# Attention: the result of each batch leaves by four indirect scatters from POOL in place of one plain store from SP

## Chip, cores and metric

The kernel runs on one core of one Trainium2 chip. The metric is device time in microseconds, the median of the runs shown; lower is better. One core has five engines that run their own lists of instructions and meet at semaphores: PE (TensorE, matmuls), DVE (VectorE), ACT (ScalarE), POOL (GpSimd) and SP (SyncE, which here only issues transfers). Transfers issued from SP and from POOL go through different queues to the same 16 DMA engines.

## What is computed

A block of a network on x of shape (16, 512, 128): half a mixture-of-experts step, attention, half a mixture-of-experts step, each on a layer norm of x and added to x. The change touches only the attention step:

```python
x = x + 0.5 * ffn(layernorm(x))          # 8 experts, top 2, and a shared one
x = x + attn(layernorm(x))
x = x + 0.5 * ffn(layernorm(x))

def attn(x, ...):                        # 16 heads of 8
    q, k, v = (x @ W.T + b for each of Wq, Wk, Wv), split by heads
    a = softmax(q k^T / sqrt(8)) * head_mask
    return (a v) @ Wo.T + bo
```

## The kernel before

The kernel is one program with three stages after a setup: `ffn1`, `attention` (L1052) and `ffn2`. Each stage goes over the 16 batches of 512 rows. Between the stages the rows lie in DRAM, in `after_ffn` and `after_attn`; a batch there is seen as 128 partitions of 4 consecutive rows (`dst_b`, L1094), so that one store moves 2 KB per partition.

In attention a batch is 16 **units** (4 quads of heads times 4 tiles of 128 rows), and a unit has two halves. For each half PE computes a pair of score tiles for the exponents (`score_exp`, L1179, rows L1187) and, 8 units ahead, a pair for the row maxima (`score_max`, L1193, rows L1201); DVE reduces the latter to maxima (`take_max`, L1482, rows L1489) and ACT takes the exponents (`exponential`, L1338, rows L1341). The maxima of a quad (group g) must be subtracted before the exponents. They are put into extra rows of the packed q operand: POOL splits them (`split_max`, L1417, rows L1423 and L1425), PE turns them (`turn_max`, L1224, rows L1227), ACT copies them out (`copy_max`, L1332, rows L1335), and POOL issues two small transfers that put them into `q_pack` (`pack_max`, L1428, rows L1432). PE waits for these transfers before the first unit of the group, in `batch` of PE (L1257):

```python
if u % NT == 0:
    g = u // NT
    pe.wait_ge(max_packed[g % 2], ...)
```

The order of every engine is written out by hand: `pieces` of PE (L1272), ACT (L1373) and DVE (L1535) and `batch` of POOL (L1441) name what goes into which unit. Work that belongs to the end of a batch is done in the early units of the next one. There, with a the batch before and b the present one: DVE normalises the last quad of a (unit 2), PE turns it and multiplies by Wo (units 3 and 4, rows L1242 and L1248), and DVE adds `x_bias` (the attention's input plus bo) and writes `x_out` (`residual`, L1506, rows L1510, unit 4). Then POOL makes the `x_bias` of b (`add_bias`, L1435, rows L1438) and packs the maxima of group 2. PE's bank `p_x` is used by many steps in turn; the semaphore `x_bank_drained` counts its uses.

SP's list for a batch (L1152) loads x for two batches on (`front.load_in`, row L344), loads the rows that the residual needs (`load_res`, row L1146), issues the packed operands of the next batch (rows L351 and L357), and last stores a (`store`, L1148, row L1150) when its residual has drained the bank. Two buffers `x_out` alternate; the residual waits until the store of two batches before has landed (`stored`, L1509). The last store follows the last residual; SP waits for all stores (L1173) before the stage is left, and all engines meet there.

Of the kernel before, what the change touches and what calls it, by code (L numbers as in the profile page):

```python
# [14 lines left out]

F32 = mybir.dt.float32
F32R = mybir.dt.float32r
BF16 = mybir.dt.bfloat16
ALU = mybir.AluOpType
ACT = mybir.ActivationFunctionType  # L20
# [2 lines left out]
P = 128  # L23
# [5 lines left out]
S = 512  # L29
NT = S // P  # L30
NB = 16
# [53 lines left out]
def need(eng, sem, value):  # L85

    if isinstance(value, int) and value <= 0:
        return
    eng.wait_ge(sem, value)
# [17 lines left out]
def every_batch(eng, batch):  # L107

    for k in range(NB):
        batch(Turn(0, k), k == 0, k == NB - 1)  # L110


def setup(nc, dram, w, feed):
# [5 lines left out]
    with ExitStack() as ctx:  # L119
# [27 lines left out]
        @block.sync  # L147
        def _(sp):
            feed.load_in(sp, begin)
            feed.load_in(sp, second)  # L150
            sp.dma_start(w.gate_w[:], dram["gate_w_t"]).then_inc(gate_w_loaded, 16)
            sp.dma_start(w.rank[:], dram["rank"]).then_inc(rank_loaded, 16)
            for dst, routed, shared, loaded in ((gate, dram["w_gate"], dram["sw_gate"], gate_loaded),
                                                (up, dram["w_up"], dram["sw_up"], up_loaded)):
                sp.dma_start(dst[:, 0:ROUTED], routed).then_inc(loaded, 16)
                sp.dma_start(dst[:, ROUTED:HID], shared).then_inc(loaded, 16)
            sp.dma_start(wq[:], dram["wq_t"]).then_inc(qk_loaded, 16)
            sp.dma_start(wk[:], dram["wk_t"]).then_inc(qk_loaded, 16)
            sp.dma_start(w.wv[:], dram["wv_t"]).then_inc(attn_loaded, 16)
            sp.dma_start(wo[:], dram["wo_t"]).then_inc(attn_loaded, 16)  # L160
            sp.dma_start(mask_rows[:], dram["head_mask"].rearrange("(p a) -> p a", a=1)).then_inc(attn_loaded, 16)
            sp.dma_start(w.bq[:], dram["bq"].rearrange("(p a) -> p a", a=1)).then_inc(attn_loaded, 16)
            sp.dma_start(w.bk[:], dram["bk"].rearrange("(p a) -> p a", a=1)).then_inc(attn_loaded, 16)
            for dst, name in ((w.bv, "bv"), (w.bo, "bo")):
                sp.dma_start(dst[:], dram[name].rearrange("(a n) -> a n", a=1)
                             .to_broadcast([P, dram[name].shape[0]])).then_inc(attn_loaded, 16)
            sp.wait_ge(attn_loaded, 16 * 7)

        @block.tensor
        def _(pe):  # L170
# [44 lines left out]
        @block.vector  # L215
        def _(dve):
            nc.vector.memset(w.minus_half[:], -0.5).then_inc(half_set, 1)
            nc.vector.memset(w.selector[:], 0.0).then_inc(selector_cleared, 1)
            feed.norm_stats(dve, begin)
            feed.norm_stats(dve, second)  # L220
            for part in range(3):
                feed.norm_var(dve, begin, part)
            for n, (_, _, full, high, low) in enumerate(splits):
                dve.wait_ge(high_done, n + 1)
                nc.vector.tensor_tensor(low, full, high.bitcast(F32), ALU.subtract).then_inc(low_done, 1)
                if n == 0:
                    dve.wait_ge(ident_loaded, 16)
                    dve.wait_ge(consts_loaded, 16)
                    nc.vector.tensor_copy(w.ident16[:], w.ident[:])
                    dve.wait_ge(selector_cleared, 1)  # L230
                    nc.vector.tensor_copy(w.selector[0:PARTS * E, :], selector[:])
                if n == 1:
                    dve.wait_ge(rank_loaded, 16)
                    for part in range(feed.EARLY_PARTS):
                        feed.route(dve, bank, begin, part)
            dve.wait_ge(attn_loaded, 16 * 7)
            nc.vector.tensor_scalar(w.wo[:], wo[:], mask_rows[:], None, ALU.mult)
            dve.wait_ge(low_done, len(splits))

# [812 lines left out]
def attention(nc, w, front, feed, src, dst):  # L1052
# [9 lines left out]
    with ExitStack() as ctx:  # L1062
# [76 lines left out]
        @block.sync  # L1139
        def _(sp):  # L1140
            def load_res(b):

                need(sp, exp_tile, b.count(PAIRS))
                sp.dma_start(x_res[b.par][:], b.of(src_b)).then_inc(x_res_loaded[b.par], 16)  # L1146

            def store(b, drained):  # L1148
                sp.wait_ge(x_bank_drained, drained)
                sp.dma_start(b.of(dst_b), x_out[b.par][:]).then_inc(stored[b.par], 16)  # L1150

            def batch(b, is_first, is_last):  # L1152
                a, c = b.step(-1), b.step(1)
                if there(b, 2):
                    front.load_in(sp, b.step(2))
                load_res(b)
                if is_last:
                    for n in following:
                        sp.wait_ge(stored[n.par], 16)
                        feed.load_in(sp, n)  # L1160
                if there(b, 1):
                    for n in range(len(PRODUCTS)):
                        front.pack_block(sp, c, "q", n)
                        front.pack_block(sp, c, "k", n)
                    front.clear_max_rows(sp, c)
                if not is_first:
                    store(a, uses(b, "out") + 1)

            end = Turn(0, NB - 1)
            every_batch(sp, batch)  # L1170
            store(end, last_uses + 3)
            for par in range(2):
                sp.wait_ge(stored[par], 16 * NB // 2)  # L1173

        @block.tensor
        def _(pe):
# [237 lines left out]
        def _(pool):  # L1414
# [20 lines left out]
            def add_bias(b, drained):  # L1435
# [2 lines left out]
                G.tensor_tensor(x_bias[:], x_res[b.par][:], w.bo[:].unsqueeze(1).to_broadcast([P, NT, D]),  # L1438
                                ALU.add).then_inc(bias_ready, 1)

            def batch(b, is_first, is_last):  # L1441
                a, c, e = b.step(-1), b.step(1), b.step(2)
                split_max(b, 1, 0 if is_first else uses(a, "m3") + 1)
# [6 lines left out]
                    front.scale(pool, e, 5 if is_first else uses(a, "x") + 1)  # L1450
                split_max(b, 2, uses(a, "m0") + 1 if not is_first else FIRST_USES.index("m0") + 1)
                add_bias(b, 0 if is_first else uses(b, "out") + 1)
                pack_max(b, 2, uses(b, "m2") + 1)
                split_max(b, 3, uses(b, "m1") + 1)
                pack_max(b, 3, uses(b, "m3") + 1)
# [10 lines left out]
                if there(e):  # L1466
                    front.operand_low(pool, e, "k")

            begin = Turn(0, 0)
            split_max(begin, 0, 0)  # L1470
            pack_max(begin, 0, FIRST_USES.index("m0") + 1)
            every_batch(pool, batch)

        @block.vector
        def _(dve):
# [30 lines left out]
            def residual(b, n):  # L1506
                dve.wait_ge(x_bank_filled, n + 1)
                dve.wait_ge(bias_ready, b.count(1, 1))
                need(dve, stored[b.par], b.half(16))  # L1509
                V.tensor_tensor(x_out[b.par][:], p_x[:].rearrange("p (t d) -> p t d", d=D), x_bias[:],  # L1510
                                ALU.add).then_inc(x_bank_drained, 1)

# [52 lines left out]
class Weights:  # L1565


    def __init__(self, nc, ctx):
# [15 lines left out]
        self.values = [sb(f"values{i}", [P, NT, HEADS, COLS]) for i in range(2)]  # L1584
        self.zeros = sb("zeros", [P, QUAD, NT])
        self.zero_rows = sb("zero_rows", [QUAD, S])


def program(nc, dram, out):
# [51 lines left out]
```

## Time and profile before

| | us |
|---|---|
| median of 3 runs | 1906.76 |
| lowest and highest | 1904.23, 1912.45 |
| span of the profiled execution | 1899.1 |
| median less that span | 7.66 |
| PE, DVE, ACT, POOL busy | 1755.1, 1391.1, 1237.0, 891.2 |

The profiled execution's own time is given by its span, from its first to its last instruction; what lies around it is the fourth line. How rows are read: in an **order of time** a row is start (us), busy time (us), engine, line of the kernel, operation, out<-in, shape, count of merged instructions, and in brackets the idle time of the engine before it and what ended that. A row of **windows** gives for a stretch its length, the busy time and count of PE, PE's weight loads, DVE, ACT and POOL, then the granted clock of PE (1.00 is 2.4 GHz), the share of the DMA engines and GB/s. A row of **DMA issues** gives the issuing queue, the count, the size of each and the median time from issue to landing. A row of a **line** gives minimum, median and maximum duration in ns, and first and last start. A row of **groups** gives count, busy us, mean ns, and idle time before. SPq rows are issues on SP's queue.

### The profile page before, as it was taken

The numbers are of one execution on the slowest core, as the hardware profiler recorded it, in microseconds if no ns is written. First come the engines' busy times: TensorE is split into PE (matmuls) and PEld (weight loads), VectorE is DVE, ScalarE is ACT, GpSimd is POOL, SyncE is SP. The second block draws the span as 40 slices with busy tenths as digits, with TensorE's granted clock in tenths as the row PEclk, the third lists the DMA queues.
The fourth block names the chain that finished last, engine by engine and source line by source line (L and its number), as shares of the span: only waits on it lengthen the run. The fifth ranks groups of instructions, "written<-read, shape, count | busy, mean of one in ns | idle before, by whom it ended". The sixth has DMA issues, their size and how long they took to land. (4 is left out here: it accounts for less than half of the span.)

```text
span 1899.1 us, 30193 instructions
## 1 busy us (share of the span) xinstructions
PE 1755.1 (92%) x9569; PEld 1100.5 (58%) x9600; DVE 1391.1 (73%) x2393; ACT 1237.0 (65%) x1914; POOL 891.2 (47%) x878
## 2 busy tenths in 40 slices
PE   5999999999968888888888888888889999999999
PEld 4887878787843333333333333333368787878776
DVE  5666766676758888888888888888457666766674
ACT  4666566656537777777777777776756566656654
POOL 5666666666732222232333322231146566656665
PEclk9999999999969999999999999999899999999999
DMA  3000100010020111111111111110001010000000
GB/s 101 23 22 25 34 22 23 21 33 22 29 81 2 53 53 54 53 54 53 53 54 53 53 42 54 53 48 24 7 28 34 23 34 12 33 22 33 11 22 12
DMA packets 42270, 69.60 MB, mean 37 GB/s; under 512 B 8508, under 2 KB 10036, under 8 KB 42164
## 3 DMA queue, kind: packets, MB, share of 16 engines
q1 hardware_dynamic: 37360, 66.20, 10.5%
q0 software_dynamic: 4096, 1.08, 0.3%
q8 instruction: 58, 0.95, 0.2%
q10 hardware_dynamic: 708, 0.98, 0.1%
q14 instruction: 48, 0.39, 0.1%
HBM read 28.36 MB, written 12.58 MB: 22 GB/s over the span
## 5 line engine op out<-in xcount | busy, mean ns | idle before, releaser
L934 POOL TENSOR_TENSOR ffn_hid_low<-ffn_hidden,ffn_hid_high 128x512 fp32r<-128x512 f32 x448 | 580.1, 1295 | 367.8 <-ACT ffn_hid_high L860 366.5
L1489 DVE TENSOR_REDUCE attn_neg_max<-attn_p_score 128x2 f32<-128x1024 f32 x512 | 623.4, 1223 | 120.1 <-PE attn_p_score L1201 118.0
L1341 ACT ACTIVATE attn_exps<-attn_p_score 128x1024 f32<-128x1024 f32 x512 | 520.4, 1025 | 217.2 <-PE attn_p_score L1187 215.4
L851 ACT ACTIVATE ffn_silu<-ffn_p_gate 128x512 f32<-128x512 f32 x448 | 266.1, 594 | 269.4 <-PE ffn_p_gate L748 267.5
L994 DVE TENSOR_TENSOR ffn_gated<-ffn_silu,ffn_p_up 128x512 f32<-128x512 f32 x352 | 241.3, 686 | 176.3 <-PE ffn_p_up L748 121.2
L860 ACT ACTIVATE ffn_hid_high<-ffn_hidden 128x512 fp32r<-128x512 f32 x448 | 280.8, 627 | 123.4 <-DVE ffn_hidden L1001 121.3
L1201 PE MATMUL attn_p_score<-k_pack,q_pack 32*128 32x512 f32 x1024 | 259.6, 506 | 53.1 <-ACT attn_exps L1341 37.4
L1218 PE MATMUL attn_p_o<-attn_exps,values 128*32 128x512 f32 x2048 | 278.0, 614 | 6.8 <-ACT attn_o_raw L1347 2.5
L1187 PE MATMUL attn_p_score<-q_pack,k_pack 32*128 32x512 f32 x1024 | 254.0, 503 | 1.5 <-DVE attn_neg_max L1489 1.5
L1001 DVE TENSOR_TENSOR ffn_hidden<-ffn_gated,ffn_p_spread 128x512 f32<-128x512 f32 x352 | 241.4, 686 | 17.8 <-remote 5.6
L1187 PEld LDWEIGHTS attn_p_score<-q_pack,k_pack 32*128 32x128 f32 x1024 | 95.1, 184 | 265.6 <-issue 236.9
L746 PE MATMUL ffn_p_gate<-feed_xt_high,gate_high 128*128 128x512 f32 x448 | 188.2, 420 | 12.8 <-POOL ffn_combine_t L974 11.7
L1432 POOL DMA_DIRECT2D q_pack<-attn_max_rows x128 | 74.6, 584 | 240.7 <-ACT attn_max_rows L1335 240.6
L746 PE MATMUL ffn_p_y<-ffn_hid_high,down_high 128*128 128x512 f32 x448 | 177.5, 396 | 2.9 <-POOL ffn_hid_low L934 2.7
L748 PE MATMUL ffn_p_up<-feed_xt_low,up_high 128*128 128x512 f32 x448 | 178.2, 398 | 0.0
L746 PE MATMUL ffn_p_up<-feed_xt_high,up_high 128*128 128x512 f32 x448 | 177.9, 397 | 0.0
L748 PE MATMUL ffn_p_gate<-feed_xt_low,gate_high 128*128 128x512 f32 x448 | 177.8, 397 | 0.0
L748 PE MATMUL ffn_p_y<-ffn_hid_low,down_high 128*128 128x512 f32 x448 | 177.2, 395 | 0.0
L747 PE MATMUL ffn_p_y<-ffn_hid_high,down_low 128*128 128x512 f32 x448 | 176.9, 395 | 0.0
L747 PE MATMUL ffn_p_gate<-feed_xt_high,gate_low 128*128 128x512 f32 x448 | 176.9, 395 | 0.0
L747 PE MATMUL ffn_p_up<-feed_xt_high,up_low 128*128 128x512 f32 x448 | 176.7, 394 | 0.0
L1201 PEld LDWEIGHTS attn_p_score<-k_pack,q_pack 32*128 32x128 f32 x1024 | 95.9, 185 | 108.2 <-ACT attn_exps L1341 91.5
(213 smaller groups left out, 2069.0 us busy)
## 6 DMA issues: line engine op xcount, KB each, us to landing
q_pack<-attn_q_high SPq DMA_DIRECT2D x32, 256.0 KB
k_pack<-attn_k_high SPq DMA_DIRECT2D x32, 256.0 KB
feed_x_in<-in_x SPq DMA_DIRECT2D x16, 256.0 KB, 2.8
ffn_x_res<-in_x SPq DMA_DIRECT2D x16, 256.0 KB, 3.4
after_ffn<-ffn_x_out SPq DMA_DIRECT2D x16, 256.0 KB, 2.0
attn_x_in<-after_ffn SPq DMA_DIRECT2D x16, 256.0 KB, 2.8
k_pack<-attn_k_low SPq DMA_DIRECT2D x16, 256.0 KB
q_pack<-attn_q_low SPq DMA_DIRECT2D x16, 256.0 KB
```

Of the source, the lines that this page charges most:

```text
L746: nc.tensor.matmul(out, weights[0], high, start=start, stop=False)
L747: nc.tensor.matmul(out, weights[1], high, start=False, stop=False)
L748: return nc.tensor.matmul(out, weights[0], low, start=False, stop=stop)
L851: nc.scalar.activation(silu[f % 2][0:n, :], p_gate[f % 2][0:n, :], ACT.Silu).then_inc(silu_ready, 1)
L860: nc.scalar.activation(hid_high[s][0:n, :], hidden[s][0:n, :], ACT.Copy).then_inc(high_ready, 1)
L934: nc.gpsimd.tensor_tensor(hid_low[s][0:n, :], hidden[s][0:n, :], hid_high[s][0:n, :].bitcast(F32), ALU.subtract).then_inc(low_ready, 1)
L1001: V.tensor_tensor(hidden[slot(b, f)][:], gated[f % 2][:], p_spread[:], ALU.mult).then_inc(weighted_ready, 1)
L1187: last = nc.tensor.matmul(score_bank("exp", b, n)[:, i, :], pack["k"][b.par][rows, g, t * P:(t + 1) * P], pack["q"][b.par][rows, g, :], st ...
L1201: last = nc.tensor.matmul(score_bank("max", b, n)[:, j % 2, :], pack["q"][b.par][rows, g, t * P:(t + 1) * P], pack["k"][b.par][rows, g, :] ...
L1218: last = nc.tensor.matmul(p_o[h * COLS:(h + 1) * COLS, :], values[b.par][:, t, g * QUAD + h, :], exps[(2 * u + h // 2) % len(exps)][:, h % ...
L1341: nc.scalar.activation(exps[n % len(exps)][:], score_bank("exp", b, n)[:], ACT.Exp, scale=inv_sqrt)\
L1489: V.tensor_reduce(neg_max[g % 2][:, j:j + 2, t], score_bank("max", b, n)[:], AX.X, ALU.max, negate=True).then_inc(max_read, 1)
```

## The change

The plain store of SP is taken out, and POOL gets `scatter_out`: four indirect transfers per batch, one for each of the 4 rows of a partition. Each writes 128 rows of 512 bytes to DRAM, to row numbers that it reads from a column of a new table `row_of` in SBUF, which setup loads. The four are placed behind `add_bias` and ahead of the packing of group 2. Each transfer raises `stored` by 16, so the waits on it count 16 * 4 per batch. The rows written, and the memory they end in, are the same.

```diff
@@ setup, SP
             sp.dma_start(w.rank[:], dram["rank"]).then_inc(rank_loaded, 16)
+            sp.dma_start(w.row_of[:], dram["row_of"]).then_inc(attn_loaded, 16)
...
-            sp.wait_ge(attn_loaded, 16 * 7)
+            sp.wait_ge(attn_loaded, 16 * 8)
@@ attention, SP
-            def store(b, drained):
-                sp.wait_ge(x_bank_drained, drained)
-                sp.dma_start(b.of(dst_b), x_out[b.par][:]).then_inc(stored[b.par], 16)
...
                     for n in following:
-                        sp.wait_ge(stored[n.par], 16)
+                        sp.wait_ge(stored[n.par], 16 * NT)
                         feed.load_in(sp, n)
...
-                if not is_first:
-                    store(a, uses(b, "out") + 1)
-
-            end = Turn(0, NB - 1)
+
             every_batch(sp, batch)
-            store(end, last_uses + 3)
             for par in range(2):
-                sp.wait_ge(stored[par], 16 * NB // 2)
+                sp.wait_ge(stored[par], 16 * NT * NB // 2)
@@ attention, POOL
+            def scatter_out(b, drained):
+                pool.wait_ge(x_bank_drained, drained)
+                for t in range(NT):
+                    at = b.k * NT + t
+                    G.indirect_dma_start(dst, bass.IndirectOffsetOnAxis(ap=w.row_of[:, at:at + 1], axis=0),
+                                         x_out[b.par][:, t, :], None).then_inc(stored[b.par], 16)
+
             def batch(b, is_first, is_last):
...
                 add_bias(b, 0 if is_first else uses(b, "out") + 1)
+                if not is_first:
+                    scatter_out(a, uses(b, "out") + 1)
                 pack_max(b, 2, uses(b, "m2") + 1)
...
             every_batch(pool, batch)
+            scatter_out(end, last_uses + 3)
@@ attention, DVE, residual
-                need(dve, stored[b.par], b.half(16))
+                need(dve, stored[b.par], b.half(16 * NT))
@@ class Weights
+        self.row_of = sb("row_of", [P, NB * NT], U32)
@@ kernel
+    p, b, t = np.arange(P)[:, None, None], np.arange(NB)[None, :, None], np.arange(NT)[None, None, :]
+    arrays["row_of"] = (b * S + p * NT + t).reshape(P, NB * NT).astype(np.uint32)
```

POOL's list in the middle of a batch before, from the second splitting of maxima to the third packing:

```order
L1423 TENSOR_TENSOR attn_max_parts<-attn_neg_max,zeros 128x16
L1425 TENSOR_TENSOR attn_max_parts<-attn_neg_max,attn_max_parts 128x16
L1438 TENSOR_TENSOR attn_x_bias<-attn_x_res,bo 128x512
L1432 DMA q_pack<-attn_max_rows 4x4x128 x2
L1423 TENSOR_TENSOR attn_max_parts<-attn_neg_max,zeros 128x16
L1425 TENSOR_TENSOR attn_max_parts<-attn_neg_max,attn_max_parts 128x16
L1432 DMA q_pack<-attn_max_rows 4x4x128 x2
```

The same place after the change (its lines are a few off, since code was added and removed above):

```order
L1417 TENSOR_TENSOR attn_max_parts<-attn_neg_max,zeros 128x16
L1419 TENSOR_TENSOR attn_max_parts<-attn_neg_max,attn_max_parts 128x16
L1432 TENSOR_TENSOR attn_x_bias<-attn_x_res,bo 128x512
L1439 DMA after_attn<-attn_x_out,row_of 8192x128 x4
L1426 DMA q_pack<-attn_max_rows 4x4x128 x2
L1417 TENSOR_TENSOR attn_max_parts<-attn_neg_max,zeros 128x16
L1419 TENSOR_TENSOR attn_max_parts<-attn_neg_max,attn_max_parts 128x16
L1426 DMA q_pack<-attn_max_rows 4x4x128 x2
```

Four transfers (their shape is shown as that of the whole target) stand between `x_bias` and the packing of group 2; the rest of POOL's order is as it was. The same four rows stand once more as POOL's last entry of the stage.

SP's list from the end of one batch into the next, before:

```order
L357 DMA q_pack<-zero_rows 4x4x512 x2
L1150 DMA after_attn<-attn_x_out 128x512
L344 DMA attn_x_in<-after_ffn 128x512
L1146 DMA attn_x_res<-after_ffn 128x512
L351 DMA q_pack<-attn_q_high 32x4x512
```

And after the change:

```order
L359 DMA q_pack<-zero_rows 4x4x512 x2
L346 DMA attn_x_in<-after_ffn 128x512
L1148 DMA attn_x_res<-after_ffn 128x512
L353 DMA q_pack<-attn_q_high 32x4x512
L353 DMA k_pack<-attn_k_high 32x4x512
```

The store is gone from SP's list, and the load of x that stood behind it follows the clearing of the packed rows directly. PE, DVE and ACT keep their lists.

## Rows read from the trace of the kernel before

**Rows 1.** The page: span, and part 1, busy us of each engine.

```profile
span 1899.1 us, 30193 instructions
...
PE 1755.1 (92%) x9569; PEld 1100.5 (58%) x9600; DVE 1391.1 (73%) x2393; ACT 1237.0 (65%) x1914; POOL 891.2 (47%) x878
```

**Rows 2.** Windows: one attention batch.

```profile
818.00:868.40 50.40, 44.78 (x306) 17.39 (x306) 42.90 (x54) 37.68 (x48) 14.57 (x23) 1.00 0.15 50
```

**Rows 3.** POOL in order of time, around the change, and in the last batch.

```profile
836.60 1.28 POOL L1438 TENSOR_TENSOR attn_x_bias<-attn_x_res,bo 128x512 f32<-128x512 f32 x1 [0.78 <-DVE attn_x_out L1510]
838.88 1.21 POOL L1432 DMA_DIRECT2D q_pack<-attn_max_rows  x2 [1.00 <-ACT attn_max_rows L1335]
845.60 0.22 POOL L1423 TENSOR_TENSOR attn_max_parts<-attn_neg_max,zeros 128x16 fp32r<-128x16 f32 x1 [5.51 <-DVE attn_neg_max L1489]
...
1342.14 1.21 POOL L1432 DMA_DIRECT2D q_pack<-attn_max_rows  x2 [1.00 <-ACT attn_max_rows L1335]
```

**Rows 4.** PE in order of time: units 7 and 8, and unit 8 of the last batch.

```profile
842.61 1.16 PE L378 MATMUL attn_p_x<-wv,attn_xt 128*128 128x128 f32 x8 [0.38 <-DVE attn_o_norm L1503]
...
845.13 0.50 PE L1187 MATMUL attn_p_score<-q_pack,k_pack 32*128 32x512 f32 x2
...
1349.86 0.50 PE L1187 MATMUL attn_p_score<-q_pack,k_pack 32*128 32x512 f32 x2
```

**Rows 5.** DMA issues of the whole run.

```profile
attn_x_in<-after_ffn SPq DMA_DIRECT2D x16, 256.0 KB, 2.8
...
after_attn<-attn_x_out SPq DMA_DIRECT2D x16, 256.0 KB, 2.0
...
q_pack<-attn_max_rows POOLq DMA_DIRECT2D x128, 8.0 KB, 1.7
...
gate_full<-in_sw_gate SPq DMA_DIRECT2D x1, 176.0 KB, 7.7
```

**Rows 6.** SP's queue in order of time, the same batch.

```profile
836.49 0.34 SPq L1150 DMA_DIRECT2D after_attn<-attn_x_out  x1
836.88 0.43 SPq L344 DMA_DIRECT2D attn_x_in<-after_ffn  x1
```

**Rows 7.** SP's queue in order of time, setup.

```profile
2.15 0.43 SPq L152 DMA_DIRECT2D rank<-in_rank  x1
...
3.15 0.43 SPq L156 DMA_DIRECT2D gate_full<-in_sw_gate  x1
```

**Rows 8.** ACT in order of time, setup.

```profile
12.89 1.66 ACT L193 ACTIVATE gate_high<-gate_full 128x1760 fp32r<-128x1760 f32 x1
```

**Rows 9.** DVE in order of time: the residual of the same batch.

```profile
835.78 0.68 DVE L1510 TENSOR_TENSOR attn_x_out<-attn_p_x,attn_x_bias 128x512 f32<-128x512 f32 x1
```

**Rows 10.** Line L1432, POOL's packing transfers: duration of an issue, and landing.

```profile
L1432 POOL DMA_DIRECT2D q_pack<-attn_max_rows x128: 569/580/754, 559.2 to 1356.3; - x128
...
DMA to landing us min/median/max: 1.7/1.7/3.1
```

**Rows 11.** The page, part 3: the queue of POOL's transfers.

```profile
q0 software_dynamic: 4096, 1.08, 0.3%
```

**Rows 12.** All engines in order of time: the end of attention.

```profile
1382.74 0.69 DVE L1510 TENSOR_TENSOR attn_x_out<-attn_p_x,attn_x_bias 128x512 f32<-128x512 f32 x1 [2.59 <-PE attn_p_x L1248]
1383.46 0.34 SPq L1150 DMA_DIRECT2D after_attn<-attn_x_out  x1
1385.96 0.95 POOL L974 MEMSET ffn_combine_t<- 128x1024 bf16 x1 [27.04 <-POOLq L1062]
```

**Rows 13.** Groups of the same batch: DVE's reductions.

```profile
L1489 DVE TENSOR_REDUCE attn_neg_max<-attn_p_score 128x2 f32<-128x1024 f32 x33 | 40.3, 1223 | 7.3 <-PE attn_p_score L1201 7.1
```

**Rows 14.** Windows: attention's last units, where no maxima are left.

```profile
1355.00:1360.00 5.00, 5.00 (x41) 2.77 (x33) 0.55 (x2) 3.86 (x6) 2.42 (x3) 1.00 0.02 3
1360.00:1365.00 5.00, 5.00 (x25) 1.23 (x25) 2.69 (x12) 2.32 (x3) 0.00 (x0) 0.52 0.00 0
```

More of the change, by code:

```diff
@@ L17 @@
 F32R = mybir.dt.float32r
+U32 = mybir.dt.uint32
 BF16 = mybir.dt.bfloat16
@@ L235, in _ @@
                         feed.route(dve, bank, begin, part)
-            dve.wait_ge(attn_loaded, 16 * 7)
+            dve.wait_ge(attn_loaded, 16 * 8)
             nc.vector.tensor_scalar(w.wo[:], wo[:], mask_rows[:], None, ALU.mult)
@@ L1146, in load_res @@
                 sp.dma_start(x_res[b.par][:], b.of(src_b)).then_inc(x_res_loaded[b.par], 16)
-            def store(b, drained):
-                sp.wait_ge(x_bank_drained, drained)
-                sp.dma_start(b.of(dst_b), x_out[b.par][:]).then_inc(stored[b.par], 16)
             def batch(b, is_first, is_last):
-                a, c = b.step(-1), b.step(1)
+                c = b.step(1)
                 if there(b, 2):
@@ L1467, in batch @@
                     front.operand_low(pool, e, "k")
-            begin = Turn(0, 0)
+            begin, end = Turn(0, 0), Turn(0, NB - 1)
             split_max(begin, 0, 0)
```

## The prediction

> **What bounds the kernel now.** Read first the span and the busy shares [rows 1]: one execution spans 1899.1 us and PE is busy 92% of it. The median of the three runs shown is 1906.76 us, 7.66 us more than the span; that part lies outside the trace, the change does not touch it, and I carry it over unchanged. The change acts inside the attention stage alone, so the next view is one attention batch by engine [rows 2]: a batch repeats every 50.4 us, PE is busy 44.78 us of it, DVE 42.90, ACT 37.68 and POOL 14.57. PE is what a batch lasts by, and POOL is idle seven tenths of the time. Idle time does not make POOL free, though: POOL works through a fixed list, and other engines wait for some of its entries. So I read POOL's own order of time around the place of the change [rows 3]: x_bias starts at 836.60 and lasts 1.28 us, POOL then idles 1.00 us, and at 838.88 it issues the two packing transfers of group 2 (1.21 us for both). The next thing on POOL starts at 845.60, after 5.51 us of idling for DVE. What ends the 1.00 us is ACT's copy of the turned maxima, named in the same row.
>
> Who needs the packing transfers? PE, before its first exponent scores of unit 8 (the unit index counts the 16 pairs of quad and tile in a batch). In PE's order of time [rows 4] the projection of the values, which belongs to unit 7, starts at 842.61, and the score pair that opens unit 8 starts at 845.13. No idle time stands in that row, so today the packing transfers are no bound there.
>
> **What is removed.** SP's store: 16 issues of 0.34 us on SP's queue [rows 6], each landing after 2.0 us [rows 5]. Nobody but SP's own list waited for it inside a batch: behind it stands only the next load of x, issued at 836.88 [rows 6] and first read in the early units of the next batch, over 40 us on. Moving that load ahead by a microsecond or two is worth nothing; those 40 us cover it, and if the cover were gone it could cost no more than its own landing of 2.8 us [rows 5]. The setup stage gets one more small load (32 KB) ahead of the gate weights on SP, about the 0.43 us of its neighbour the rank load [rows 7]. The later half of the gate weights is issued at 3.15 and lands 7.7 us on [rows 5, 7], at 10.9, and ACT touches them at 12.89 [rows 8]: hidden, cost nothing, and 0.43 us once if that cover were gone.
>
> **What is added.** POOL now issues four scatters per batch between x_bias and the packing transfers. Their wait is the one x_bias has already passed (the drain of the same residual, whose DVE row starts at 835.78 and lasts 0.68 us [rows 9]), so they add no wait, only their issue time. No row shows an indirect transfer, so I bound the issue time X of one. The only transfers POOL issues today are the 128 packing transfers: 569 to 754 ns, median 580 [rows 10]. They move 16 rows of 512 B each, and their queue shows 4096 packets for 128 of them, 32 each [rows 11], which I read as 16 rows and 16 completions. Low end: all of it is fixed, X = 0.58 us. Middle: it goes with packets, 128 + 16 = 144 against 32, a factor 4.5, X = 2.6 us. High end: it goes with rows, a factor 8, X = 4.6 us. POOL's smallest compute instruction takes 0.22 us [rows 3], so part of the 0.58 is surely fixed. I take X = 1.4 us: 0.35 us of it fixed and the remaining 0.23 us growing 4.5 times (0.35 + 1.04). It stands nearer the low row because that row is of the same queue and has the same 16 completions. It is an estimate and the weakest number here.
>
> The Trainium skill ("DMA: Bandwidth & Descriptors", Anatomy of one DMA) states that descriptor generation is small and that many descriptors can be emitted before the added cost shows. By that rule X stays at the low end; no run here shows it yet, and it is rival B below.
>
> **How much POOL can be late.** Today the second packing transfer starts issuing at 838.88 + 0.58 = 839.46 and lands 1.7 us later [rows 10], at 841.2 if that is counted from the start of the issue, 841.7 from its end. PE wants it at 845.13, which leaves 3.9 to 3.4 us. Add the 1.00 us that POOL idles before it, and four scatters may take 4.9 to 4.4 us; I take 4.6. The break-even is X = 1.15 us. Behind the packing transfers POOL's next entry, the maxima of group 3, is due at 845.60; with X = 1.4 POOL is free at 837.9 + 5.6 + 1.2 = 844.7, so it is not late. The residual's own wait on the store of two batches before, and the DMA share of 0.15 [rows 2], are far from mattering.
>
> **The sum.** 4 x 1.4 = 5.6 us against 4.6: PE stands 1.0 us at unit 8. PE runs in order and is the bound, so I count this in full. It happens in the 14 batches from the second to the fifteenth: 14.0 us. In the last batch PE reaches unit 8 at 1349.86 after packing at 1342.14 [rows 3, 4], 7.72 us against 845.13 - 838.88 = 6.25, so it has 1.5 us more margin and loses nothing. The packing transfers also queue behind 64 KB scatters on POOL's one queue; I count zero for this, and up to 1 us a batch (14 us) goes into the range.
>
> At the end of attention nothing covers the store. Today the last residual ends at 1383.43, SP issues the store at 1383.46, and the next stage's first instruction starts at 1385.96 [rows 12]: the store's 2.0 us and 0.5 us behind it. With scatters the last of four ends its issue 5.6 us after the residual and lands 1.1 us (1.7 - 0.58) or more later, 6.7 against 2.0: about 5 us more. Sum 14 + 5 = 19 us: 1899.1 + 19 = 1918 us of span, and 1906.76 + 19 = **1926 us**.
>
> **Rivals.** A run is told from no change here from about 0.5%, 9.5 us, on.
>
> *B, the margin holds (not slower).* If X is at most 1.1 us, four scatters fit into the 4.6 us and PE never waits. Only the end is left: 4 x 0.58 + 1.1 - 2.0 = 1.4 us at the low end, 3.5 us at X = 1.1. That gives 1908 to 1910 us. For it speaks the 0.58 us row, which includes all 16 completions; against it, eight times the rows and a list of row numbers that POOL must read. The point from which it decides is X = 1.15.
>
> *C, issue goes with rows or packets.* At X = 2.6 us PE waits 10.4 - 4.6 = 5.8 us in 14 batches (81 us), 10.4 - 6.1 = 4.3 us in the last, and the end grows by 10.4 + 1.1 - 2.0 = 9.5 us: 95 us, 2002 us. At X = 4.6 the same sum gives 14 x 13.8 + 12.3 + 17.5 = 223 us, 2130 us. Another road here is that POOL's issue has to wait while DVE works, an instruction of 1.22 us at a time [rows 13]: X = 0.58 + 1.22 = 1.8 us, which gives 14 x 2.6 + 1.1 + 6.3 = 44 us, 1951 us. Against that road: today's 128 issues spread only from 569 to 754 ns beside a DVE that is busy 85% of the batch. The Trainium skill ("SBUF — State Buffer", SBUF: two separate sides) states that transfers issued from GpSimd cannot write descriptors while DVE runs in a two-port mode; by that rule this road would be open, and the trace's narrow spread does not show it for DVE's reductions. A PE that stands longer in every batch might also lose its clock: once only half the scores were left at the end of attention, the granted clock went from 1.00 (2.4 GHz) to 0.52 (1.2 GHz) [rows 14]. I give that no price; it would come on top of C.
>
> *D, faster.* Only SP's 16 short issues go away, and no row shows PE waiting for SP. A gain would have to come from outside the trace.
>
> **How the numbers follow.** Forecast (X between 1.15 and about 1.9): 0.50. B: 0.28. C (X above 1.9): 0.20. D: 0.02. Slower by over 0.5% takes the forecast and C, 0.70; within 0.5% is B, 0.28; faster 0.02. The likeliest case alone reaches from about 1914 (X = 1.2) to 1955 us (X = 1.9, 14 x 3.0 + 1.5 + 6.7 = 50 us). The range adds B below, down to 1907, and the cheaper part of C above, X = 2.4: 14 x 5.0 + 3.5 + 8.7 = 82 us, 1989 us.
>
> **What would show it.** In the changed profile POOL's scatters should have rows of about 1.4 us, 64 of them. The idle time of PE (or its weight loads) at the score pair of unit 8 should be put down to POOL's packing transfer or appear as a gap of about 1 us in each batch, and the batch should repeat every 51.4 us. The stretch from the last residual to the next stage's first instruction should grow from 2.5 to about 7.5 us. The prediction is wrong in size if the scatter rows are far from 1.4 us; it is wrong in mechanism if they are above 1.2 us and the batch still takes 50.4 us, or if the batch grows with no gap at unit 8.

## The result, and the profile after

| | before | after |
|---|---|---|
| median, us | 1905.49 (4 runs) | 1924.03 (4 runs) |
| lowest and highest | 1903.85, 1912.45 | 1912.02, 1929.64 |
| ratio, 95% interval | | 1.0077 [1.0039, 1.0114] |
| span of the profiled execution | 1899.1 | 1923.2 |
| mean granted clock of PE | 0.985 | 0.976 |

The changed kernel is slower by 18.5 us in the median; the ratio stands for 14.7 us, its interval for about 7 to 22 us. The two profiled executions differ by 24.1 us, which is more, and a part of that is not the change's, as the first-batch rows will show. Where one execution has both a time and a span, 1924.98 and 1923.2 us here, 1.7 to 2.0 us lie outside the span. So the profiled execution before took about 1901 us, and most of the 7.66 us that the table before puts outside the trace is the difference between executions; the prediction, which adds to the median, does not suffer from it. Four places answer to the four steps of the prediction.

**POOL around the change**, in order of time in one batch (it answers to [rows 3]):

```profile
842.62 1.28 POOL L1432 TENSOR_TENSOR attn_x_bias<-attn_x_res,bo 128x512 f32<-128x512 f32 x1 [0.76 <-DVE attn_x_out L1514]
844.07 1.11 POOL L1439 DMA_INDIRECT after_attn<-attn_x_out,row_of  x1 [0.17 <-issue]
845.49 1.00 POOL L1439 DMA_INDIRECT after_attn<-attn_x_out,row_of  x1 [0.30 <-issue]
846.79 0.95 POOL L1439 DMA_INDIRECT after_attn<-attn_x_out,row_of  x1 [0.30 <-issue]
848.05 0.96 POOL L1439 DMA_INDIRECT after_attn<-attn_x_out,row_of  x1 [0.30 <-issue]
849.01 1.27 POOL L1426 DMA_DIRECT2D q_pack<-attn_max_rows  x2
851.60 0.22 POOL L1417 TENSOR_TENSOR attn_max_parts<-attn_neg_max,zeros 128x16 fp32r<-128x16 f32 x1 [1.31 <-DVE attn_neg_max L1493]
```

Packing began 1.00 us after the end of `x_bias` before; now it begins 849.01 - 843.90 = 5.11 us after it, 4.11 us later. Each scatter is 0.95 to 1.11 us of busy time, and before it stand 0.17 or 0.30 us in which POOL waited for nothing that the profile shows. All 64, and their landing, by line:

```profile
L1439 POOL DMA_INDIRECT after_attn<-attn_x_out,row_of x64: 954/976/1113, 641.4 to 1402.3; - x64
...
DMA to landing us min/median/max: 2.2/2.3/4.3
```

The Trainium skill ("DMA: Bandwidth & Descriptors", Anatomy of one DMA) gives a transfer on this path about 2.0 us plus its bytes over 436 GB/s, by which an estimate for 64 KB is 2.15 us. The 2.3 us of the row is close to it, while the 1.7 us of the 8 KB packing transfers [rows 10] lies below its constant part. The page's row of POOL's queue (part 3 of the page) stood at 4096 packets in [rows 11]:

```profile
q0 software_dynamic: 6144, 5.28, 0.9%
```

That is 2048 more for 64 scatters, **32 each**, as many as a packing transfer has, although a scatter moves 128 rows.

**PE at unit 8**, the same batch, in order of time, where [rows 4] showed no idle time:

```profile
849.71 0.50 PE L1181 MATMUL attn_p_score<-q_pack,k_pack 32*128 32x512 f32 x2
...
851.49 0.50 PE L1181 MATMUL attn_p_score<-q_pack,k_pack 32*128 32x512 f32 x2 [0.28 <-DMA q_pack<-attn_max_rows]
```

A gap has appeared where the prediction put it, put down to POOL's packing transfer; PE stands 0.28 us in this batch. Over the run, in the view of waits:

```profile
PEld attn_p_score L1181 <- DMA q_pack<-attn_max_rows: 18.3, 14, 2.5
PE attn_p_score L1181 <- DMA q_pack<-attn_max_rows: 5.6, 14, 1.6
```

(us in all, times, longest.) Fourteen times, as the prediction counted; the weight load ahead of the scores carries the larger figure, but the batches did not grow by as much. What a batch lost is read better from its length, from one start of POOL's `x_bias` to the next. The next `x_bias` after the rows above, and the next before, after the one at 836.60 of [rows 3]:

```profile
893.33 1.28 POOL L1432 TENSOR_TENSOR attn_x_bias<-attn_x_res,bo 128x512 f32<-128x512 f32 x1 [0.76 <-DVE attn_x_out L1514]
```

```profile
886.97 1.28 POOL L1438 TENSOR_TENSOR attn_x_bias<-attn_x_res,bo 128x512 f32<-128x512 f32 x1 [0.78 <-DVE attn_x_out L1510]
```

A batch now repeats every 50.66 to 50.71 us in most places, **50.68** in the middle, against 50.37 before: 0.31 us more. Two batches lost more, 54.53 us (the seventh to the eighth `x_bias`, 893.33 to 947.86) and 52.00 us (998.52 to 1050.52). In both the packing transfers landed late, after 2.4 and 2.6 us, and in the first PE's clock fell behind the gap. Rows of the first one's DMA view, from the start of the packing to 3 us behind it:

```profile
q8 instruction: 1, 0.02, 2.6%
...
q_pack<-attn_max_rows POOLq DMA_DIRECT2D x2, 8.0 KB, 2.4
```

Besides POOL's transfers the DMA engines moved one packet there of the queue that the profile calls instruction, q8, and so they did in the other late batch. In the twelve other packings of the fourteen no packet of q8 falls into these 3 us, and they land after 1.7 to 1.8 us. That this packet delays them is not shown by a run of its own. The two gaps in PE's order of time, and windows around the first:

```profile
903.04 0.50 PE L1181 MATMUL attn_p_score<-q_pack,k_pack 32*128 32x512 f32 x2 [1.12 <-DMA q_pack<-attn_max_rows]
...
1008.67 0.50 PE L1181 MATMUL attn_p_score<-q_pack,k_pack 32*128 32x512 f32 x2 [1.55 <-DMA q_pack<-attn_max_rows]
```

```profile
900.00:904.00 4.00, 2.88 (x25) 1.26 (x23) 2.61 (x4) 1.46 (x3) 1.42 (x4) 1.00 0.09 25
904.00:906.00 2.00, 1.89 (x14) 0.53 (x12) 1.65 (x2) 2.00 (x3) 0.00 (x0) 0.85 0.01 4
906.00:910.00 4.00, 3.93 (x17) 1.16 (x17) 2.21 (x3) 2.58 (x5) 0.00 (x0) 0.50 0.00 0
...
914.00:916.00 2.00, 2.00 (x12) 0.22 (x8) 1.62 (x3) 0.82 (x1) 0.92 (x1) 0.59 0.00 0
916.00:918.00 2.00, 2.00 (x15) 1.01 (x15) 1.37 (x2) 1.48 (x2) 0.00 (x0) 1.00 0.00 0
```

The clock is the third figure from the end: 1.00 (2.4 GHz) until the gap, 0.50 (1.2 GHz) for some 10 us behind it. The 1.55 us gap of the other batch left no such mark, so a gap of this size does not always bring the clock down.

**The end of attention** (it answers to [rows 12]), DVE's residual, POOL in order of time, and the instructions of the line at which all engines meet:

```profile
1397.41 0.69 DVE L1514 TENSOR_TENSOR attn_x_out<-attn_p_x,attn_x_bias 128x512 f32<-128x512 f32 x1 [2.59 <-PE attn_p_x L1242]
```

```profile
1398.40 1.05 POOL L1439 DMA_INDIRECT after_attn<-attn_x_out,row_of  x1 [22.20 <-DVE attn_x_out L1514]
...
1402.32 0.95 POOL L1439 DMA_INDIRECT after_attn<-attn_x_out,row_of  x1 [0.30 <-issue]
1410.13 0.95 POOL L976 MEMSET ffn_combine_t<- 128x1024 bf16 x1 [6.86 <-POOLq L1064]
```

```profile
L1064 POOLq DRAIN  x1: 11735/11735/11735, 1398.2 to 1398.2; - x1
L1064 SPq COMPARE_BRANCH  x1: 38/38/38, 1404.6 to 1404.6; - x1
L1064 SPq EVENT_SEMAPHORE  x1: 17/17/17, 1410.1 to 1410.1; - x1
```

From the end of the residual (1398.10) to the next stage it is 12.03 us, against 2.53 before. SP's wait for the stores is over at 1404.6, 6.5 us after the residual. But POOL's own drain, the instruction with which an engine leaves the stage, lasts until 1398.2 + 11.7 = 1409.9, 6.7 us after the end of the last issue. In the kernel before, the row of the same drain is as long and nobody saw it, since it begins 28 us before the end (both rows count what POOL's engine was still busy with: four scatters after, one TENSOR_TENSOR of 1.26 us before):

```profile
L1062 POOLq DRAIN  x1: 11855/11855/11855, 1357.6 to 1357.6; - x1
```

**The first batch** is not the change's. Its clock came up to 1.00 later; windows of after, then of before:

```profile
580.00:590.00 10.00, 9.24 (x43) 2.29 (x41) 5.93 (x6) 4.57 (x7) 4.70 (x7) 0.50 0.00 0
590.00:600.00 10.00, 9.62 (x63) 4.15 (x56) 7.17 (x9) 5.12 (x5) 1.63 (x4) 0.76 0.02 3
```

```profile
570.00:580.00 10.00, 8.59 (x45) 2.53 (x49) 7.99 (x17) 6.48 (x8) 1.15 (x2) 0.75 0.01 2
580.00:590.00 10.00, 8.74 (x65) 2.80 (x57) 8.31 (x8) 6.58 (x9) 5.91 (x8) 1.00 0.01 3
```

The first two `x_bias` stand 56.1 us apart after and 51.3 before. No scatter has been issued by then, and of the ten experiments below two show the short form (both have scatters) and eight the long one (two of them have no scatter at all). So these 4.8 us come and go from one execution to the next.

The 24.1 us of span are then: first batch 4.8; fourteen batches 14 x 0.31 = 4.3 by their common length, and 3.9 + 1.3 = 5.2 more in the two late ones (from the second `x_bias` to the last it is 714.18 us against 704.71, 9.5 in all); end of the stage 9.5; 0.3 left over. Without the first batch that is 19 us, beside 18.5 in the medians. The last batch adds little here: from its `x_bias` to its residual it took 42.9 us before and 43.3 after. But it took 41 to 49 us in the experiments below, with and without scatters, so a loss of a few us there could not be read from one execution.

### The profile page after: what moved, and what is told of

Its sections match the earlier page's. It is cut to its first block and busy times, and to the rows that moved or that the text cites. A ratio compares the mean times of both kernels' runs of the same rounds, so it can differ in the third digit from the quotient of the medians.

```text
span 1923.2 us, 30242 instructions
## 1 busy us (share of the span) xinstructions
PE 1763.5 (92%) x9569; PEld 1099.3 (57%) x9600; DVE 1391.8 (72%) x2393; ACT 1238.4 (64%) x1914; POOL 955.1 (50%) x942
## 5 line engine op out<-in xcount | busy, mean ns | idle before, releaser
L1195 PE MATMUL attn_p_score<-k_pack,q_pack 32*128 32x512 f32 x1024 | 263.5, 514 | 56.9 <-ACT attn_exps L1335 41.4
L1212 PE MATMUL attn_p_o<-attn_exps,values 128*32 128x512 f32 x2048 | 283.5, 626 | 7.8 <-ACT attn_o_raw L1341 3.0
```

The costliest lines, as they stand in the source:

```text
L1195: last = nc.tensor.matmul(score_bank("max", b, n)[:, j % 2, :], pack["q"][b.par][rows, g, t * P:(t + 1) * P], pack["k"][b.par][rows, g, :] ...
L1212: last = nc.tensor.matmul(p_o[h * COLS:(h + 1) * COLS, :], values[b.par][:, t, g * QUAD + h, :], exps[(2 * u + h // 2) % len(exps)][:, h % ...
```

## Experiments

The theory at this point (A): the gap at unit 8 comes from POOL reaching the packing late, and the rest is the end of the stage, where POOL leaves last. Its rivals: the scatters slow the packing transfer in the queue they share, and the end is the landing of the scatters. Each term has its own run.

### The scatters behind the packing

```diff
-                if not is_first:
-                    scatter_out(a, uses(b, "out") + 1)
                 pack_max(b, 2, uses(b, "m2") + 1)
+                if not is_first:
+                    scatter_out(a, uses(b, "out") + 1)
```

> The four scatters of a batch move one place on in POOL's list, behind the packing of group 2, where POOL idles 5.5 us. Theory A (the scatters' issue time makes the packing late): the gap of PE at unit 8 goes, a batch repeats every 50.4 us again, and with it go the stretches of lower clock that follow a long gap; the end of the stage keeps its 12 us between the last residual and the next stage. About 1915 us, 9 to 10 above before. Theory B (the scatters' traffic or their landing slows the batches, wherever they stand): the batch stays at 50.7 us, about 1924 us. Theory C (what the profile shows is mostly the clock of the stage's first batch, which has no scatter): no change against the changed kernel beyond its spread.

Measured: 1915.02 us against 1905.96, ratio 1.0053 [1.0029, 1.0076]. Batches of 50.35 us, also the two that had been late, and in the waits of PE and its weight loads one entry of 0.8 us is left of fourteen. The end takes 11.84 us. So the order on POOL makes the whole loss inside the batches, and the end is a loss by itself, 9.3 us by its length (11.84 less 2.53).

### The last batch stored by SP

```diff
-            scatter_out(end, last_uses + 3)
...
+            sp.wait_ge(x_bank_drained, last_uses + 3)
+            sp.dma_start(Turn(0, NB - 1).of(dst_b), x_out[1][:]).then_inc(stored_last, 16)
```

> The scatters stay ahead of the packing, but the last batch is stored by SP in one plain store. Theory A (at the end of the stage a transfer from POOL is paid with its issue, its landing and POOL's drain behind it, 9.5 us more than the plain store): the stretch from the last residual to the next stage falls from 12.0 to 2.5 us, the batches stay at 50.7 us, about 1914 us. Rival (POOL's drain takes its 11 us after any use of its queue, whoever stores last): the stretch stays near 12 us only if POOL is busy with transfers just before, which it is not here, so this rival too gives 2.5 us; what would speak against A is a stretch above 5 us.

Measured: 1913.44 us, ratio 1.0040 [1.0020, 1.0060]. The end is back at 2.55 us; batches of 50.63 to 50.70 us, with 51.80 and 51.54 in two, the seventh and the ninth as in the changed kernel, but with the clock at 1.00 behind their gaps. So the same order on POOL cost 6.1 us from the second `x_bias` to the last here (710.77 against 704.71) where it cost 9.5 in the execution above: most of the rest is the one fall of the clock. The excesses of this run and of the one before, 0.40% and 0.53%, add up to 0.93%; the change had 0.77% [0.39, 1.14].

### Both

> Both edits together. Theory A (two costs and no third): within 0.3% of before, batch 50.4 us, end 2.5 us, about 1905.5 us. If the scatters cost something else, by their traffic or on another engine, it stays above 1909 us.

The two edits together: 1906.33 us, ratio 0.9997 [0.9972, 1.0022], batches of 50.36 us, end 2.55 us. Sixty scatters are still issued, and no loss is left that this interval can tell, about 5 us either way. None of the kernels here beats the one before.

### POOL late, without a scatter

From the kernel before, with four additions into a tile that nobody reads, of 1.28 us or so each, where the scatters would stand:

```diff
                 add_bias(b, 0 if is_first else uses(b, "out") + 1)
+                if not is_first:
+                    for n in range(4):
+                        need(pool, idle_done, (b.k - 1) * 4 + n)
+                        G.tensor_tensor(idle_out[:], x_res[b.par][:], w.bo[:]..., ALU.add).then_inc(idle_done, 1)
                 pack_max(b, 2, uses(b, "m2") + 1)
```

> The kernel before with SP's plain stores, and on POOL four additions of the size of x_bias (1.28 us each) into a spare tile in place of the scatters: POOL is late by about 5.4 us with no transfer at all. Theory A: PE gets a gap at unit 8 of about 0.3 to 0.7 us in 14 batches, the end stays at 2.5 us, 1909 to 1916 us. Theory B (queueing of the packing behind the scatters on POOL's queue makes the gap): no gap, 1905.5 us.

Measured: 1912.67 us, ratio 1.0026 [1.0002, 1.0050]. Batches of 50.80 us, the end unchanged. POOL in order of time:

```profile
844.50 5.42 POOL L1457 TENSOR_TENSOR attn_idle_out<-attn_x_res,bo 128x512 f32<-128x512 f32 x4
849.85 1.21 POOL L1433 DMA_DIRECT2D q_pack<-attn_max_rows  x2
```

and the waits of PE:

```profile
PE attn_p_score L1188 <- DMA q_pack<-attn_max_rows: 6.2, 14, 1.0
PEld attn_p_score L1188 <- DMA q_pack<-attn_max_rows: 18.9, 14, 1.9
```

The same fourteen waits, 6.2 us against 5.6, with nothing ahead of the packing in the queue. The rival of the shared queue falls for the batches: it is time on POOL that counts. Here packing starts 5.3 us after `x_bias` and the batch is 0.43 us longer; with the scatters 5.1 us gave 0.31.

### More lateness

The same four additions put into the changed kernel, ahead of the scatters, so that POOL is about 10 us late.

```diff
                 if not is_first:
+                    for n in range(4):
+                        need(pool, idle_done, (b.k - 1) * 4 + n)
+                        G.tensor_tensor(idle_out[:], x_res[b.par][:], w.bo[:]..., ALU.add).then_inc(idle_done, 1)
                     scatter_out(a, uses(b, "out") + 1)
```

> The changed kernel with four additions of the size of x_bias (1.28 us each) more ahead of the scatters: POOL is later by another 5.4 us in 15 batches. Theory A (the gap grows one to one with the lateness, and nothing absorbs it): the gap at unit 8 is 5.5 to 5.9 us, a batch 56 us, the whole 1924 + 14 x 5.4 + 4 = about 2000 us. With the clock falling behind the longer gap in each batch, by the 3.8 us that the one dip in the changed kernel's trace cost: 2050 us. If PE catches up after the gap: below 1980 us.

Measured: 2041.34 us, ratio 1.0713 [1.0675, 1.0750], mean granted clock 0.938. This is near the 2050 us expected with a loss of clock behind each gap, not the 2000 without. Batches take 57.2 to 60.5 us, the one ahead of the last `x_bias` 66.1, where the added POOL time alone would give about 56. PE at unit 8, and windows of the same stretch:

```profile
883.61 0.79 PE L1182 MATMUL attn_p_score<-q_pack,k_pack 32*128 32x512 f32 x2 [5.61 <-DMA q_pack<-attn_max_rows]
```

```profile
870.00:875.00 5.00, 4.82 (x36) 1.60 (x34) 4.21 (x5) 3.43 (x5) 4.76 (x5) 1.00 0.00 0
875.00:880.00 5.00, 2.62 (x24) 1.32 (x20) 3.27 (x5) 2.05 (x2) 4.12 (x4) 1.00 0.08 26
880.00:885.00 5.00, 1.39 (x7) 0.96 (x8) 0.52 (x1) 0.56 (x1) 2.68 (x5) 0.67 0.09 30
885.00:890.00 5.00, 4.95 (x22) 1.35 (x20) 2.95 (x3) 3.04 (x5) 0.00 (x0) 0.50 0.00 0
890.00:900.00 10.00, 9.99 (x45) 3.59 (x49) 5.83 (x8) 5.39 (x8) 2.41 (x3) 0.56 0.02 3
900.00:910.00 10.00, 9.35 (x64) 3.36 (x56) 7.94 (x7) 9.21 (x13) 3.71 (x6) 1.00 0.01 2
```

PE waits 5.61 us, the clock falls from 1.00 to 0.50 and is back at 1.00 in the row from 900 on, some 17 us later. PE waited 81.4 us in 15 batches, 5.4 each, and a batch is 7 to 10 us longer than the 50.37 before. The rest goes with the clock: its mean over a batch is 0.86 to 0.94 (0.74 in the one of 66.1 us), against 1.00 before. With gaps of this length a microsecond of POOL cost more than one.

### What a scatter's time goes by

From the kernel with the scatters behind the packing, three more scatters in each batch, of 64, 32 and 16 rows, into an array that nobody reads.

```diff
+                for t, rows in enumerate((64, 32, 16)):
+                    at = b.k * NT + t
+                    G.indirect_dma_start(spare, bass.IndirectOffsetOnAxis(ap=w.row_of[0:rows, at:at + 1], axis=0),
+                                         x_out[b.par][0:rows, t, :], None).then_inc(stored[b.par], 16)
```

> Scatters behind the packing, and three more per batch of 64, 32 and 16 rows into a spare array, to read the issue time by rows. By the prediction's split (0.35 us fixed, the rest with packets) 64 rows take about 0.6 of the time of 128 and 16 rows a third or less; if the time is mostly fixed, all three stand near 0.9 us. POOL is held 8 to 9 us behind the packing, 2 to 3 us longer than it idles there, so a batch may grow by up to that.

One execution: 1913.56 us. POOL in order of time, the last of the four and the three:

```profile
848.59 0.96 POOL L1439 DMA_INDIRECT after_attn<-attn_x_out,row_of  x1 [0.30 <-issue]
849.85 0.91 POOL L1443 DMA_INDIRECT spare<-attn_x_out,row_of  x1 [0.30 <-issue]
851.06 0.87 POOL L1443 DMA_INDIRECT spare<-attn_x_out,row_of  x1 [0.30 <-issue]
852.24 0.85 POOL L1443 DMA_INDIRECT spare<-attn_x_out,row_of  x1 [0.30 <-issue]
```

128, 64, 32 and 16 rows take 0.96, 0.91, 0.87 and 0.85 us: about 0.85 us is fixed and a row adds 1 ns. The short ones make 32 packets each as well (7680 in the queue, 1536 more for 48 of them), so the packets do not go by the rows. Batches stay at 50.36 us, so over 8 us of POOL's time behind the packing cost nothing, though the expectation left room for 2 to 3 us a batch. The end took 10.75 us from the residual.

### The end: plain transfers, and what the drain goes by

One plain store of 256 KB by POOL in place of the four scatters, in all batches:

```diff
-                for t in range(NT):
-                    at = b.k * NT + t
-                    G.indirect_dma_start(...).then_inc(stored[b.par], 16)
+                G.dma_start(b.of(dst_b), x_out[b.par][:]).then_inc(stored[b.par], 16)
```

> POOL issues one plain store of 256 KB per batch in place of the four scatters, at the same places. Theory A (what counts in the batches is how long POOL is held, what counts at the end is POOL's drain): one issue of under 1.5 us is far below the 4.6 us of margin, so no gap at unit 8 and a batch of 50.4 us; the end of the stage still pays the drain, which took 6 to 10.5 us behind POOL's last entry in the runs so far, so 9 to 13 us from the last residual to the next stage against 2.5: 1912 to 1917 us. Rival (the long end belongs to indirect transfers or their landing, not to POOL's drain): 3 to 5 us at the end, about 1907 us.

Measured: 1905.80 us, ratio 1.0002 [0.9978, 1.0026]; an issue takes 646 ns, batches are 50.36 us. The end takes 4.26 us, not the 9 us and more that theory A gave it with a drain of the same length:

```profile
L1064 POOLq DRAIN  x1: 3726/3726/3726, 1394.5 to 1394.5; - x1
```

So "POOL's drain takes 11.7 us behind its transfers" was too simple. Three more kernels vary what is issued in the stage and what is issued last, in one execution each. The first has scatters behind the packing and stores the last batch alone by one plain transfer of POOL:

```diff
-            scatter_out(end, last_uses + 3)
+            pool.wait_ge(x_bank_drained, last_uses + 3)
+            G.dma_start(end.of(dst_b), x_out[1][:]).then_inc(stored[1], 16)
```

> Scatters behind the packing in the 14 batches, as in the run of that name; the last batch alone is stored by one plain transfer that POOL issues. Disputed is what POOL's drain at the end of the attention stage goes by: it took 11.7 us from the last residual with four scatters there, and 3.7 us with one plain transfer there and plain transfers in all batches. Theory S (it goes with what was issued last): as with plain transfers everywhere, drain about 3.7 us, residual to the next stage about 4.3 us. Theory H (it goes with what was issued in the whole stage, 60 scatters here): the drain stays long, 7 us or more, and the end takes 8 to 10 us.

The second has plain transfers of POOL everywhere and scatters the last batch alone:

```diff
+            for t in range(NT):
+                at = (NB - 1) * NT + t
+                G.indirect_dma_start(dst, bass.IndirectOffsetOnAxis(ap=w.row_of[:, at:at + 1], axis=0),
+                                     x_out[1][:, t, :], None).then_inc(stored[1], 16)
```

> Plain transfers from POOL in 15 batches, four scatters in the last batch alone. Theory S: drain about 11.7 us and 12 us from the residual to the next stage, as in the changed kernel. Theory H: with four scatters in the whole stage the drain is that of plain transfers, ending about 3 us after the last issue, so some 4 x 1.28 + 3.1 = 8 us from the residual. Batches of 50.36 us in both.

The third is the first again, but its last batch leaves by one scatter of POOL and a store of SP for the other three rows of each partition:

```diff
+            G.indirect_dma_start(..., x_out[1][:, NT - 1, :], None).then_inc(stored[1], 16)
...
+            sp.dma_start(Turn(0, NB - 1).of(dst_b)[:, 0:NT - 1, :], x_out[1][:, 0:NT - 1, :]).then_inc(stored_last, 16)
```

> Scatters behind the packing; in the last batch SP stores three quarters and POOL scatters one quarter. Theory S with a fixed part: 6.2 to 6.7 us of drain behind the end of that one issue, so 1.1 + 6.5 + 0.7 = about 8.3 us from the residual to the next stage. Theory S with a part for each scatter (a quarter of what is left of 6.5 us beyond the 3.1 us that one plain transfer leaves): about 1.1 + 4 + 0.7 = 5.8 us.

Whole times were 1909.69, 1914.89 and 1911.75 us beside 1912.66 of the kernel before; single executions do not tell these apart.

POOL's drain in the three, in this order:

```profile
L1064 POOLq DRAIN  x1: 6825/6825/6825, 1386.9 to 1386.9; - x1
```

```profile
L1064 POOLq DRAIN  x1: 8128/8128/8128, 1391.2 to 1391.2; - x1
```

```profile
L1064 POOLq DRAIN  x1: 7488/7488/7488, 1388.5 to 1388.5; - x1
```

| transfers of POOL in the stage, beside 128 packings | last issue | drain behind its end, us | residual to next stage, us |
|---|---|---|---|
| 64 scatters (the change) | 4 scatters | 6.7 | 12.0 |
| 64 scatters, behind the packing | 4 scatters | 6.5 | 11.8 |
| 61 scatters | 1 scatter | 6.2 | 7.8 |
| 60 scatters, 1 plain | 1 plain | 6.2 | 7.4 |
| 15 plain, 4 scatters | 4 scatters | 2.9 | 8.4 |
| 16 plain | 1 plain | 3.1 | 4.3 |
| 64 scatters, 48 short ones | 7 scatters | 1.8 | 10.8 |

(The drain's start plus its length, less the end of the last issue.) The first theory, that what is issued last sets the drain, falls twice: one plain transfer behind 60 scatters is followed by 6.2 us, four scatters behind plain transfers by 2.9. What POOL issued in the whole stage matters. The drain behind one plain transfer was a little shorter than theory H gave (6.8 us against 7 or more, 7.4 against 8 to 10 for the whole end). One scatter at the end came to 7.8 us, near the 8.3 expected of a fixed part and far from the 5.8 expected of a part for each scatter. It is not simply more with more transfers: 112 scatters leave 1.8 us, and the kernel before, with the packings alone, has POOL's last instruction (1.26 us from 1357.66) end 10.5 us before its drain does, at 1369.5; the run with additions alone shows the same 10.5. Nor is the drain a wait for a transfer on its way: in the two kernels whose last batch SP stores, with 60 scatters, POOL's last instruction is a TENSOR_TENSOR. It ends 2 to 3 us behind the last issue of a packing, which with its 1.7 to 2.0 us has landed by then, and the drain lasts 6.2 to 6.3 us behind it all the same. What exactly the drain has to work off is left open; no run here settles it.

## Why the prediction came out

1926 us was forecast and 1924.03 measured; the forecast's sum was 14 + 5 = 19 us, and the two profiled executions show about 9.5 + 9.5, the run with SP's last store only 6.1 in the batches. The two places and the way each comes about for PE were right; that the total came within 2 us was luck. Two errors had opposite signs, and medians of four runs with an interval of about 7 to 22 us cannot test 19 more closely. With the measured 5.1 us in place of 5.6, the forecast's own sum would have been 14 x 0.5 + 5.1 + 1.1 - 2.0 = 11 us, 1918 us. (Its upper end of the likeliest case, 1955 us at X = 1.9, is 1957 by its own 50 us; nothing hangs on it.)

- **The issue, X = 1.4 us.** One scatter costs POOL 0.98 + 0.30 = 1.28 us, and four hold the packing back until 5.1 us behind `x_bias`, where 5.6 were taken. The size was nearly right, the working was not. 0.35 us fixed and 0.23 us growing 4.5 times with packets is wrong in both halves: the packets are 32 again, and 0.85 us are fixed. The step that failed is "128 + 16 = 144 packets"; it took a row of the target for a packet. The Trainium skill's rule in rival B ("DMA: Bandwidth & Descriptors", Anatomy of one DMA), that many descriptors can be emitted before the added cost shows, agrees with 0.85 to 0.96 us from 16 to 128 rows. The low end that B drew from it, X = 0.58, failed: an indirect issue of 16 rows takes 0.85 us, where a plain one of as many bytes takes 0.58.
- **The margin, 4.6 us.** POOL's 5.11 us cost 0.31 us a batch, so the margin is 4.8 us if PE pays the excess in full, inside the bounds of 4.4 and 4.9 and near the end at which landing is counted from the start of the issue. The stall of 1.0 us was a small difference of two large numbers, and came out as 0.3: 4.3 us in fourteen batches instead of 14. The mechanism, its place and the count of 14 were right, and the run with idle additions shows it without any scatter.
- **What was not on the list: late landings and the clock.** Two batches lost 3.9 and 1.3 us more. The landing of packing has a maximum of 3.1 us against a median of 1.7, and this stood in [rows 10] already; the prediction used the median alone. Before, packings at this place landed late too, after 2.3 us at 687.79 and 2.4 at 1141.08, and their batches kept 50.36 and 50.37 us, since the margin took it; with none left it reaches PE. The fall of the clock was named, without a price, in rival C only. Here it came behind a gap of 1.12 us.
- **The queue shared with 64 KB scatters**, counted at nothing: right, the additions without scatters do the same.
- **The end, +5 us.** It is +9.5. The landing was right: SP's wait ends 6.5 us after the residual, against 6.7 forecast. The step that failed is "nothing covers the store", which took the store for the last thing to wait for. POOL's drain was in the trace of before, 11.9 us long, but it began 28 us ahead of the end; giving POOL the last transfers of the stage took its cover away. The prediction asked what the moved instructions cost and not what POOL does when it has issued them.
- **The last batch, 0, and setup, 0.** In the last batch PE waits for no packing after the change either, and the first `x_bias` starts at 583.84 us against 583.82, so setup and the stage before attention cost nothing.
- **Rival C's second road**, issues that wait for DVE (1.8 us): all 64 lie between 0.95 and 1.11 us, and the 0.30 us ahead of them is as steady, so it is not seen here.

## What to carry to other kernels

Before something is put on an engine that looks idle, find the next entry of its list that another engine waits for, take the margin from the latest landing in the trace and not from the median, and put the new work behind that entry: here the same scatters cost 0.31 us a batch and two late landings ahead of the packing and nothing behind it. At the end of a stage, look at how each engine leaves it: an engine's drain that began 28 us before the end, and so was hidden, became the last thing to end once the engine had the stage's last work. Where plain addresses will do, one plain store from POOL (646 ns to issue) did the work of four scatters (5.1 us) at no loss that an interval of a quarter of a percent could tell.

## What was not expected of the hardware

- An indirect issue is almost all fixed cost: 0.85 us for 16 rows and 0.96 for 128, with 0.30 us before each when they follow one another; 16 rows of 512 bytes and 128 rows alike made 32 packets.
- POOL's drain after a stage with transfers of its own took from 1.8 to 10.5 us behind its last instruction, and this went by what POOL had issued in the whole stage, not by what it issued last nor by how long ago; by what count is open.
- The late landings of packing came in the same two batches after the change, in the run with SP's last store and in the one with additions alone, the seventh to eighth and the ninth to tenth. In all six places one packet of the queue called instruction, q8, moved within 3 us of the packing's issue; that it is the cause is not shown, nor why it comes there.
- A gap of 1.12 us in PE was followed by some 10 us at 0.50 clock, while one of 1.55 us was not, and waits of 5.4 us in every batch made batches longer by 7 to 10.
